# Hybrid block on one core: batch 0's state recurrence moved to VectorE and TensorE, weight low parts to GpSimd, one C row block asked for earlier

## What is computed

```python
x = x + ssm(layernorm(x))
x = x + ffn(layernorm(x))
x = x + attn(layernorm(x))
x = x + ffn(layernorm(x))

# ssm, per batch: 64 channels c, 8 states s
xb, zb = silu(dwconv3(x @ W_in.T)) split in halves
dt, b, c = split(xb @ W_xproj.T);  b, c = tanh(b), tanh(c)
delta = clip(softplus(dt @ W_dt.T + b_dt), 1e-4, 1)
decay = clip(exp(-delta * a), 1e-4, 1)          # a = softplus(A_log) + 1e-4
state[t] = decay * state[t-1] + (1 - decay) * b * xb
y[t] = sum_s(state * c) + D * xb
out = concat(y, zb) @ W_out.T

# ffn: 8 experts, 128 -> 512 -> 128, all computed, mixed by the product of two softmaxes
# attn: 16 heads of 8; a row sees its chunk of 10 and 25 rows to the left
```

## Time and profile before

| | us |
|---|---|
| median of three runs | 1640.91 |
| the profiled execution, its own time | 1642.63 |
| its span, first to last instruction | 1640.8 |
| PE busy (share) | 1545.5 (94%) |
| DVE busy | 1021.3 (62%) |
| ACT busy | 953.3 (58%) |
| POOL busy | 411.3 (25%) |

### The profile page before, as it was taken

One profiled execution on the slowest core, in us unless ns is written; L12 is line 12 of the kernel. 1 busy time (PEld: TensorE's weight loads), 2 busy tenths in 40 slices (PEclk: granted clock), 3 DMA queues, 4 the chain that ended last, 5 costly groups with the idle time before them and its releaser, 6 DMA issues. The chain is left out here.

```text
span 1640.8 us, 31286 instructions
## 1 busy us (share of the span) xinstructions
PE 1545.5 (94%) x12484; PEld 1293.3 (79%) x12484; DVE 1021.3 (62%) x2316; ACT 953.3 (58%) x1306; POOL 411.3 (25%) x403
## 2 busy tenths in 40 slices
PE   5399969999999999999999999999999999999998
PEld 2278857788878888787888878887788888887887
DVE  5556638656676667666675676667756665576543
ACT  6273737854678466846666586467744664366421
POOL 5332232322223222133320342123401221122000
PEclk9999989999999999999999999999999999999999
DMA  5000120002001200021000300030002000200000
GB/s 186 13 36 31 53 90 1 36 19 78 8 1 54 80 18 2 12 88 45 8 2 25 116 5 8 2 111 33 1 1 78 8 1 1 78 8 2 1 7 7
DMA packets 40961, 55.48 MB, mean 34 GB/s; under 512 B 2560, under 2 KB 18944, under 8 KB 40816
## 3 DMA queue, kind: packets, MB, share of 16 engines
q1 hardware_dynamic: 40816, 53.48, 9.5%
HBM read 42.75 MB, written 10.72 MB: 33 GB/s over the span
## 5 line engine op out<-in xcount | busy, mean ns | idle before, releaser
L965 ACT ACTIVATE h<-pg 128x512 f32<-128x512 f32 x512 | 304.5, 598 | 569.4 <-PE pg L263 567.2
L909 PE MATMUL pd<-w_down,h 128*128 128x128 f32 x4096 | 537.4, 280 | 0.8 <-DVE x L991 0.8
L909 PEld LDWEIGHTS pd<-w_down,h 128*128 128x128 f32 x4096 | 504.1, 192 | 31.0 <-issue 9.5
L1011 DVE TENSOR_TENSOR h<-h,pu 128x512 f32<-128x512 f32 x512 | 346.4, 679 | 175.0 <-PE pu L263 173.6
L816 POOL TENSOR_TENSOR att_arena<-att_arena 100x500 f32<-100x500 f32 (+2 forms) x192 | 172.9, 900 | 597.1 <-DVE att_arena L747 589.3
L261 PE MATMUL pg<-ffn_x_hi,w_gate_hi 128*128 128x512 f32 x512 | 247.1, 483 | 0.0
L261 PE MATMUL pu<-ffn_x_hi,w_up_hi 128*128 128x512 f32 x512 | 205.8, 402 | 15.4 <-DVE h L1011 15.2
L262 PE MATMUL pu<-ffn_x_lo,w_up_hi 128*128 128x512 f32 x512 | 204.1, 399 | 0.0
L262 PE MATMUL pg<-ffn_x_lo,w_gate_hi 128*128 128x512 f32 x512 | 204.0, 399 | 0.0
L263 PE MATMUL pg<-ffn_x_hi,w_gate_lo 128*128 128x512 f32 x512 | 203.8, 398 | 0.0
L263 PE MATMUL pu<-ffn_x_hi,w_up_lo 128*128 128x512 f32 x512 | 203.7, 398 | 0.0
(11 more groups left out here) (170 smaller groups left out, 1758.6 us busy)
## 6 DMA issues: line engine op xcount, KB each, us to landing
arena<-bc_spread SPq DMA_DIRECT2D x56, 256.0 KB
qk_rows<-qk_parts SPq DMA_DIRECT2D x32, 256.0 KB, 2.3
q<-qk_rows SPq DMA_DIRECT2D x32, 256.0 KB, 3.7
k<-qk_rows SPq DMA_DIRECT2D x32, 256.0 KB, 4.4
arena<-in_x SPq DMA_DIRECT2D x8, 256.0 KB, 2.8
x<-in_x SPq DMA_DIRECT2D x8, 256.0 KB, 3.1
h<-in_w_gate SPq DMA_DIRECT2D x8, 256.0 KB, 6.5
h<-in_w_up SPq DMA_DIRECT2D x8, 256.0 KB, 2.7
```

The lines of the kernel that those rows point to most:

```text
L909: last = nc.tensor.matmul(pd[:, t * P:(t + 1) * P], h_b[:, d % NH, t * P:(t + 1) * P], wd[:, d % NCH, :], start=d % CPE == 0 and t == 0, s ...
L965: nc.scalar.activation(h_b[:, c % NH, :], pg[c % 2][:, :], ACT.Silu).then_inc(gate_done, 1)
L1011: nc.vector.tensor_tensor(h, h, pu[d % 2][:, :], ALU.mult).then_inc(h_done, 1)
```

## The change

- **Batch 0's four state tiles** get a slot of `dec` each (`dec_0`: the two of `dec`, and the buffers of x of batches 2 and 3, not loaded yet). ScalarE computes the four exps in a row, then D times x into `ctile[0]`. VectorE clips, forms (decay - 1) times x, multiplies by B straight from PSUM, scans, multiplies by C from PSUM: 20 instructions in an order written by hand. GpSimd has no part in it.
- **B and C** are split in a high and a low part (in `qk_s`, where the selection matrix stands now as well) and spread with two fast matmuls each into eight places of PSUM, all at once. The raw B and C rows go to `pd`, so they no longer wait for the bank of `delta`.
- **The sum over k** is left to TensorE, which accumulates the projections of D x and of the four tiles in one bank.
- **Weight low parts** are all GpSimd's. ScalarE's casts of tiles 7 to 15 stand behind the exps.
- **Head of a pass:** the transposes wait for one normalised piece each. For pass 0 the cast for the feed-forward comes before the float32 copy, `T_HEAD[0]` goes from -9 to -4.5, so routing stands behind the first gate chunk and batch 1's normalisation ahead of it.
- **C2 of batch 2** is asked for one slot earlier, which puts it in front of the copies of q and k.

```diff
-T_HEAD = [-9, 25] + [NCH * m - 8 for m in range(2, NM)]
+T_HEAD = [-4.5, 25] + [NCH * m - 8 for m in range(2, NM)]
...
-        return dict(ln=-33, win=-31, dt=-26, k=(-24, -21.5, -19, -16.5), y=-10.5)
+        return dict(ln=-33, win=-31, dt=-26, k=(-24, -23, -22, -21), y=-19)
...
+        dec_0 = [dec[:, 0, :], dec[:, 1, :]] + [xb[i][:, :, :].rearrange("p t d -> p (t d)") for i in (2, 3)]
...
+        b_ps, c_ps = (pg[0], pg[1], pd, att_ps[1]), (pu[0], pu[1], att_ps[0], pg[0])
...
-            pe.wait_ge(ln_sems[kind][2], TT * (k + 1))
             for t in range(TT):
+                pe.wait_ge(ln_sems[kind][2], TT * k + t + 1)
...
                     for k in range(KT):
+                        for row, bank in ((2 * k, b_ps[k]), (DSTATE + 2 * k, c_ps[k])):
+                            if k == KT - 1 and bank is c_ps[k]:
+                                pe.wait_ge(b_used, 1)
+                            for v in range(2):
+                                last = nc.tensor.matmul(bank[:, :], sel[:, row * INNER:(row + 2) * INNER], bc_part[v],
+                                                        start=v == 0, stop=v == 1)
+                            last.then_inc(bc_full, 1)
...
+                    for k in range(KT):
+                        nc.scalar.activation(dec_0[k], delta, ACT.Exp, scale=neg_a[:, k:k + 1]).then_inc(dec_exp, 1)
+                    nc.scalar.activation(ctile[0], xb2, ACT.Copy, scale=pk("d_skip")).then_inc(dx_done, 1)
+                    return
...
+                    def clip(k):
+                        dve.wait_ge(dec_exp, k + 1)
+                        link.count(nc.vector.tensor_scalar(dec_0[k], dec_0[k], 1e-4, 1.0, ALU.max, ALU.min))
+                        clipped[k] = link.n
+                    def with_x(k):
...
+                        link.count(nc.vector.scalar_tensor_tensor(btile[k % 2], dec_0[k], 1.0, xb2, ALU.subtract, ALU.mult))
+                    def with_b(k):
...
+                        nc.vector.tensor_tensor(btile[k % 2], btile[k % 2], b_ps[k][:, :], ALU.mult).then_inc(b_used, 1)
+                    def scan(k):
...
+                    def with_c(k):
...
+                        nc.vector.tensor_tensor(dec_0[k], dec_0[k], c_ps[k][:, :], ALU.mult).then_inc(y_done, 1)
...
-                    yield at["k"][k]
+                    yield at["k"][k] - (1 if i == 2 else 0)
                     sp.wait_ge(y_done, n - 1)
                     sp.dma_start(ctile[k % 2], bc_r[DSTATE + 2 * k:DSTATE + 2 * k + 2, :].unsqueeze(1)
...
-                        if 0 <= j < 2 * E and j % 2 == 0:
+                        if 0 <= j < 2 * E:
                             split_w(j)
```

More of the change, by code:

```diff
@@ L309, in pe @@
                 name = ("route", m)
+                pe.wait_ge(fx_f32, m + 1)
                 ps = b.take(pe, name)
-                pe.wait_ge(fx_f32, m + 1)
                 for t in range(TT):
@@ L407, in pe @@
                                      pk("w_out_z")[0:INNER, :], start=t == 0, stop=False)
-                pe.wait_ge(y_done, KT * (i + 1))
-                for t in range(TT):
-                    last = nc.tensor.matmul(ps[:, t * P:(t + 1) * P], tot[:, t * P:(t + 1) * P], pk("w_out_y"),
-                                            start=False, stop=t == TT - 1)
+                parts = [tot]
+                if i == 0:
+                    pe.wait_ge(dx_done, 1)
+                    parts = [ctile[0]] + dec_0
+                else:
+                    pe.wait_ge(y_done, KT * (i + 1))
+                for k, part in enumerate(parts):
+                    if i == 0 and k:
+                        pe.wait_ge(y_done, k)
+                    for t in range(TT):
+                        last = nc.tensor.matmul(ps[:, t * P:(t + 1) * P], part[:, t * P:(t + 1) * P], pk("w_out_y"),
+                                                start=False, stop=(k, t) == (len(parts) - 1, TT - 1))
                 b.fill(last, ("y", i))
@@ L486, in total @@
-                def total(k):
-                    dve.wait_ge(y_part, KT * i + k + 1)
-                    if k == 0:
-                        ins = nc.vector.scalar_tensor_tensor(tot, xb2, pk("d_skip"), ctile[0], ALU.mult, ALU.add)
-                    else:
-                        dve.wait_ge(y_done, KT * i + k)
-                        ins = nc.vector.tensor_tensor(tot, tot, ctile[k % 2], ALU.add)
-                    ins.then_inc(y_done, 1)
[L496 to L500, removed]
-                    if i and k == 0:
-                        yield at["k"][k] + 5
-                        total(k)
@@ L538, in pool @@
                 norm_pool(pool, link, "ssm_ln", i)
-                def with_b(k):
-                    pool.wait_ge(b_moved[k % 2], 16 * ((KT * i + k) // 2 + 1))
-                    nc.gpsimd.tensor_tensor(btile[k % 2], btile[k % 2], xb2, ALU.mult).then_inc(bx_done, 1)
-                def clip(k):
-                    d = dec[:, k % 2, :]
+                if i == 0:
+                    return
+                for k in range(KT):
+                    n = KT * (i - 1) + k
+                    d, bt, ct = dec[:, k % 2, :], btile[k % 2], ctile[k % 2]
+                    yield at["k"][k] + 1.5
```

172 lines of the change are left out of this document (102 added, 70 removed).

## The result

The changed kernel takes 1627.88 us (median of 4 executions, 1626.91 to 1629.89) where the kernel before takes 1642.39 (4 executions, 1638.66 to 1644.30): a ratio of 0.9914, 95% interval 0.9895 to 0.9933. So it is faster, by 14.5 us; 18.2 were forecast. The profiled execution is the slowest of the four, 1629.89 with a span of 1628.1.

A forecast was written before the change was run, and what follows sets the result against it. Set-up was taken as a chain through ScalarE, GpSimd and VectorE, the rest as TensorE's. States 13.5, head 4.7 and C2 0 sum to 18.2 us off 1642.63, 1624.4; less 1.7 for the median, 1622.7, range 1617 to 1630.

The forecast's parts named there:

- The end of the states: Batch 0's set-up: VectorE's last product with C ends at 45.6 us, between 41.1 and 49.9.
- The seven waits: Batch 0's states: VectorE instructions with all operands in SBUF wait for GpSimd's turns, 4.5 us after early hand-overs.
- Rival 1: Batch 0's states: GpSimd hardly disturbs VectorE, states end at 41.1, kernel at 1617.9 us; chance 0.12.
- The residual add: After batch 0's states: at 48.3 instead of 61.80 us, 13.5 us earlier (bounds 18.5 and 9.2).
- The head: Start of pass 0, to batch 1's input projection: 4.7 us saved (2.6 to 5.5) by transposes, cast, a removed wait and pace.
- Rival 3: First 20 chunks: batch 1's chain of transfers sets the pace, the head's 4.7 us are lost, 1627.4 us; chance 0.07.
- Weights: Set-up: GpSimd's low parts end at about 47 us and down weights are in by 46, both hidden by 8 us.
- Rival 4: Set-up: GpSimd becomes the bound, first chunk waits for all 16 low parts, kernel at about 1649 us; chance 0.03.
- C2: Batch 2's transfer of C ahead of the q and k copies: 0 us, with -1 to +1.5 for the loads' share.
- Rival 2: Batch 2: C2 holds q and k back in full, attention and B3 start 5.1 us later, 1627.8 us; chance 0.10.
- something unforeseen: An unknown in the larger part of the set-up that costs some us; chance 0.04.
- The size of the hole: At 200 to 240 us, batch 2: TensorE's wait of 7.48 us hangs on B3 and stays unchanged.

The follow-up runs named there:

- e3: Changed kernel with GpSimd's low parts of weight tiles 8 to 15 held until batch 0's fourth scan: 1629.85 us, one execution.
- e4: Changed kernel with the head of pass 0 put back as before (routing and norm order, transposes, copy ahead of cast): 1632.05 us, ratio 0.9931 to the kernel before.
- e1: Changed kernel with C2 of batch 2 back behind the copies of q and k: 1625.88 us, ratio 0.9897 to the kernel before.
- e6: Kernel before with C2 of batch 2 ahead of the copies of q and k as its only edit: 1642.55 us, ratio 1.0003.
- e8: Changed kernel with one row of B or C per transfer and C2 of batch 2 behind the copies again: 1602.09 us, ratio 0.9753 to the kernel before.
- e2: Changed kernel with each two-row fan-out of B and C sent as two one-row transfers to 64 partitions: 1601.93 us, ratio 0.9754 to the kernel before.
- e9: Changed kernel with 16 idle matmuls added in a TensorE wait of the set-up, shifting its code fetches: 1630.35 us, ratio 0.9925 to the kernel before.

## Why the prediction held, and where it did not

**The end of the states: right in time, by two errors that cancel.** The last product with C was put at 45.6 and ended at 45.61. The seven waits that were laid out, 1.2, 0.5, 0.5, 0.7, 0.6, 0.4 and 1.2 (5.1 in all), came as 1.1, 0.4, 0.5, 1.1, 0.4, 0.5 and 1.1 (5.05), taking e3's undisturbed durations (scan 1.21, product with x 0.68, clip 0.41). The 0.6 us that the prediction took off for early hand-overs did not come: the contention, forecast at 4.5, was 5.0. What hid it is a first exp at 26.3 instead of 26.7, and that is chance. The mechanism holds: three scans beside GpSimd take 2.27 to 2.30 and one 1.69, products with x 1.11 to 1.16, products with B and C 0.65 to 0.69, so these run freely. Rival 1 (no contention) falls by e3.

**The residual add: 0.5 late in the sum.** 47.78 instead of 48.3, as the attention weights' instructions met only the end of GpSimd's last turn (the first cast took 0.51, the others 0.23): its sixteenth part ended at 45.95, ahead of 47. The 0.5 us I took for that was the wrong choice within its bounds. The states give 14.0 instead of 13.5; of these 0.5 are chance, as the first loads landed that much sooner (6.74 against 7.26).

**The head: right in kind, 0.6 to 0.8 too large.** Forecast 4.7; against the kernel before it gives 3.9 (20.4 to 16.5), by e4 4.1 to 4.2. From the residual add to the first gate chunk it took 6.6 us (forecast 6.4), and from there to batch 1's projection 9.9 instead of 12.7: the 2.1 of the wait and 0.7 of pace. The term that was mis-sized is the pace, 1.3 forecast and 0.7 measured: the records stay near 0.63 us until 61.79, seven us after the first gate chunk. Rival 3 falls: the lead at chunk 24 is 17.6 of 17.9.

**Weights: right.** The one wait for a raw weight tile, ScalarE's of 0.53 us at 34.17, held nothing up: GpSimd had tiles until its last part ended. Rival 4 falls.

**C2: the mechanism right, the balance off by 1.4.** C2's product on GpSimd started at 195.99, forecast about 195. The copies finish later and the loads catch up, but with 1.1 to 1.4 us missing, near my upper bound of +1.5. Rival 2's 5.1 us fall. The step that failed is "they were done at 222.2, and would again be": in the changed kernel they were done 1.1 to 1.4 us later against the stream (e1, e6). Why they don't catch up in full is not shown. Since B3 follows the loads, it was late by the same amount. The times don't establish the cost (e6), and with quick transfers it is none (e8).

**What was missing from the sum.** "Later than that the streams are equal but for SP" was false for one stream no view of instructions shows: TensorE's code. Its packets moved against batch 6's write, and the stall there with the stretch at half clock behind it (908.7) took 3.5 us of the lead. The forecast gave a chance to "something unforeseen" in the set-up alone. So for the two profiled executions: 14.0 + 3.9 = 17.9, less 0.3 by chunk 24, less 1.3 at the hole (C2; e1 and e6 have 1.4), plus 1.5 and less 1.6 for a half-clock stretch in either, less 3.5 at batch 6, is 12.7, and the spans differ by that (1640.8 - 1628.1). The medians differ by 14.5, since the profiled executions are not the median ones. The range of 1617 to 1630 held; the centre was 5.2 us too low, and the narrower 1620 to 1626 was missed. Of these 5.2, 1.5 is the kernel before itself, whose median over four executions is 1642.39 and not 1640.91; the other 3.7 is less than the 4.8 that the stall at batch 6 and C2 took between the two traces, a difference within the scatter of the executions. By its number, 1627.88 looks like rival 2 (1627.8) or rival 3 (1627.4), and both are refuted: that is coincidence.

**The size of the hole.** The prediction called it unchanged, and it was, but for C2's 1.3. That transfers cost more in it than the whole change wins (15.4 us at the hole and 26 in all by e2, against 14.5) could have been asked of its own reading, "lands each 5.1 us, one after another", which went no further than C2's place.

## What to carry to other kernels

Before moving a transfer ahead of others, ask why it takes as long as it does. Here a fan-out of two rows that lands in 5.1 us was worth 1.4 us by its place in the queue and 20 to 26 us by its shape. For contention between VectorE and GpSimd a layout turn by turn, with the instructions that have a PSUM operand as free turns, gave the sum of the waits within 0.1 us (5.1 against 5.05); the deduction from it was the error. And a lead is best followed chunk by chunk through both traces: with a second trace of the same kernel beside them, it tells a loss of the change from a loss by chance, which spans and medians of few executions don't.

## What the runs showed of the hardware

A packet of what I take for TensorE's code (16 KB, 0.9 to 1.6 us on one DMA engine) that started 0.05 to 0.63 us behind a 32 KB write went with a landing of 2.1 to 2.9 us instead of 1.6, thirteen times of thirteen. Which write is hit changed with the number of TensorE's instructions ahead (e9), so an edit in the set-up can cost time 850 us later. The Trainium skill's page "Runtime: NRT & Kernel Launch", section "Instruction fetch mechanics", describes code that comes in 16 KB blocks of 256 instructions by DMA, its cost mostly hidden; the size and the spacing agree with the trace, but behind batch 6's write the cost was not hidden.

A stretch of 3.4 us with the granted clock at half level, in the middle of dense work, costs 1.5 to 1.6 us and falls in one execution and not in another (469.7 and 869.1 in the first trace of the kernel before, both absent in the second; 1434.4 in the changed kernel, absent in e1, e3 and e4). Two traces of one kernel differ by 3.1 us through two of these (spans 1640.8 and 1637.7), a fifth of what the change is worth. The stretch at 908.7, behind the wait at 906, came in each of the four traces that have this wait.
